# Attention kernel: P V of a group of heads in one block instead of two, and other tiles moved by ScalarE

## The reference

```
q = layer_norm(x) @ wq + bq;  k = ctx @ wk + bk;  v = ctx @ wv + bv      # 16 heads of 32
s = (q . k) / sqrt(32), with -inf where the key's position is behind the query's
o = softmax(s) @ v;  x1 = x + o @ wo + bo
out = x1 + gelu(layer_norm(x1) @ w1 + b1) @ w2 + b2                      # 512 -> 2048 -> 512
```

## Time and profile before

| | us |
|---|---|
| median of 3 runs | 2786.91 (2784.9 to 2787.2) |
| the profiled execution, its own time | 2783.56 |
| its span | 2781.8 |
| TensorE busy | 2739.5 (98%) |
| TensorE weight loads busy | 2501.3 (90%) |
| VectorE busy | 2016.4 (72%) |
| ScalarE busy | 1674.5 (60%) |
| GpSimd busy | 362.6 (13%) |
| mean granted TensorE clock | 0.997 of full |

### The profile page before, as it was taken

One profiled execution on the slowest core, in us unless ns is written; L12 is line 12 of the kernel. 1 busy time (PEld: TensorE's weight loads), 2 busy tenths in 40 slices (PEclk: granted clock), 3 DMA queues, 4 the chain that ended last, 5 costly groups with the idle time before them and its releaser, 6 DMA issues.

```text
span 2781.8 us, 65798 instructions
## 1 busy us (share of the span) xinstructions
PE 2739.5 (98%) x22056; PEld 2501.3 (90%) x22056; DVE 2016.4 (72%) x4853; ACT 1674.5 (60%) x4049; POOL 362.6 (13%) x362
## 2 busy tenths in 40 slices
PE   8999999999999999999979999999998999999999
PEld 7888888888888888888869999999998999999999
DVE  7777777777777776777688787787778666566556
ACT  5766667666676666766666556556556444444444
POOL 2222222221232212322110000000000000000000
PEclk9999999999999999999999999999999999999999
DMA  5333233332333323333243534434435433343342
GB/s 186 119 133 128 98 124 121 132 126 100 124 121 130 124 105 121 119 130 127 100 163 130 196 130 164 189 130 172 182 127 206 157 143 137 134 166 136 120 159 99
DMA packets 153018, 383.03 MB, mean 138 GB/s; under 512 B 13440, under 2 KB 17536, under 8 KB 144768
## 3 DMA queue, kind: packets, MB, share of 16 engines
q1 hardware_dynamic: 152960, 382.28, 37.0%
HBM read 172.51 MB, written 109.05 MB: 101 GB/s over the span
## 4 chain that ended last, share of the span: by engine, by line
PE 95%; DVE 2%; issue 1%; ACT 1%; DMA 0%; POOL 0%; SPq 0%; DVEq 0%; ACTq 0%; POOLq 0%
PE bank_d L478 19%; PE bank_t L505 11%; PE bank_d L473 6%; PE bank_s L1247 6%; PE bank_s L1248 6%; PE bank_s L1249 6%; PE bank_s L493 6%; PE bank_v L528 5%; PE bank_d L1247 5%; PE bank_d L1249 5%; PE bank_d L1248 5%; PE bank_v L1247 2%; PE bank_v L1248 2%; PE bank_v L1249 2%; PE bank_t L1247 1%
## 5 line engine op out<-in xcount | busy, mean ns | idle before, releaser
L824 ACT ACTIVATE sm<-sm,mins 128x128 f32<-128x128 f32 (+3 forms) x1024 | 572.1, 559 | 428.7 <-DVE mins L650 423.5
L650 DVE CUSTOM_DVE_ANT_0 sm<-bank_s,mask 128x128 f32<-128x128 f32 (+3 forms) x1024 | 475.2, 484 | 95.3 <-PE bank_s L493 92.9
L595 DVE COPY pT<-bank_t 128x384 f32<-128x384 f32 (+1 forms) x544 | 307.4, 565 | 230.8 <-PE bank_t L505 230.8
L1247 PE MATMUL bank_s<-w_hi,a_hi 128*128 128x256 f32 x1536 | 435.9, 284 | 3.5 <-DVE a_lo L1373 3.5
L1248 PE MATMUL bank_s<-w_lo,a_hi 128*128 128x256 f32 x1536 | 435.3, 283 | 0.0
L1249 PE MATMUL bank_s<-w_hi,a_lo 128*128 128x256 f32 x1536 | 435.3, 283 | 0.0
L505 PE MATMUL bank_t<-ident,sm 128*128 128x128 f32 x2560 | 412.4, 275 | 8.2 <-ACT pT L595 3.7
L505 PEld LDWEIGHTS bank_t<-ident,sm 128*128 128x128 f32 x2560 | 307.1, 140 | 88.5 <-issue 32.4
L1247 PE MATMUL bank_d<-b_hi,w_hi 128*128 128x256 f32 x1280 | 368.8, 288 | 14.3 <-ACT g L1674 7.0
L1249 PE MATMUL bank_d<-b_hi,w_lo 128*128 128x256 f32 x1280 | 363.6, 284 | 0.0
L1248 PE MATMUL bank_d<-b_lo,w_hi 128*128 128x256 f32 x1280 | 363.3, 284 | 0.0
(11 more groups left out here) (158 smaller groups left out, 6371.2 us busy)
## 6 DMA issues: line engine op xcount, KB each, us to landing
stack<-st_hi SPq DMA_DIRECT2D x256, 256.0 KB, 2.4
stack<-st_lo SPq DMA_DIRECT2D x128, 256.0 KB, 2.4
xr<-x_scratch SPq DMA_DIRECT2D x64, 512.0 KB, 4.2
b_scratch<-b_hi SPq DMA_DIRECT2D x16, 1792.0 KB, 9.1
b_scratch<-b_lo SPq DMA_DIRECT2D x16, 1792.0 KB, 12.8
b_hi<-b_scratch SPq DMA_DIRECT2D x16, 1792.0 KB, 7.4
b_lo<-b_scratch SPq DMA_DIRECT2D x16, 1792.0 KB, 11.1
xt<-in_x SPq DMA_DIRECT2D x64, 256.0 KB, 2.6
```

The source lines that it names most:

```text
L595: copy(out, src).then_inc(moved[n % 2], 1)
L650: op = V.tensor_tensor_reduce(sm[:, n % SLOTS_S, off:off + w], bank_s[n % BANKS_S][:, off:off + w], mask[:, 512 - w:512], 1.0, 0.0, ALU.ad ...
L824: op = A.activation(row, row, ACT.Exp, bias=mins[:, g % 2, c:c + 1], scale=-1.0, accum_out=sums[:, g % 2, c:c + 1])
L1247: pe.matmul(o, lh, rh, start=opens, stop=False, skip_group_check=True)
```

## The change

P V of both pairs of group g is issued in step 3 of group g+1, behind the step's dense matmuls and ahead of its transposes. No matmul is added or dropped. The block needs tile 11, the last of its group, whose transposes are in step 2 and whose move is at the beginning of VectorE's or ScalarE's step 3. ScalarE now moves tiles 3, 5, 9 (3, 5, 7, 9 in group 2) and VectorE the others, tile 11 among them.

```diff
-ACT_MOVES = [(5, 9, 11), (5, 9, 11), (3, 5, 7, 9, 11), (5, 9, 11)]
+ACT_MOVES = [(3, 5, 9), (3, 5, 9), (3, 5, 7, 9), (3, 5, 9)]
...
-    R_AT, PV1_AT, PV0_AT, O_PROD_AT, O_HIGH_AT, O_HIGH_LATE = 4, 5, 9, 6, 7, 11
+    R_AT, PV_AT, O_PROD_AT, O_HIGH_AT, O_HIGH_LATE = 4, 3, 6, 7, 11
...
                     for job, i, j in steps:
                         dense_step(it, job, g, i, j)
-                    if k == PV1_AT and not (it.first and g == 0):
+                    if k == PV_AT and not (it.first and g == 0):
+                        pv(it, g - 1, 0)
                         pv(it, g - 1, 1)
-                    if k == PV0_AT and not it.tail:
-                        pv(it, g, 0)
                     if n >= LAG and not it.tail or n < LAG and not it.first:
                         p_transpose(it, n - LAG)
```

## The result

The changed kernel takes 2819.06 us (median, 2816.67 to 2819.47) against 2787.05 for the one before: 1.0115 of it, 95% interval 1.010 to 1.013. Forecast were 2812 us, in a range of 2784 to 2826. Spans of the profiled executions: 2815.0 and 2781.8, so 33.2 us are to be found. In a trace of any of these kernels the first score stands either some 32.5 or some 36 us after the start (32.6 before, 32.5 in the changed kernel, 36.4 in e8), and the run times fall into two such groups some 3 us apart, so that where few us matter I compare executions with the same start.

What follows compares the result with a forecast made beforehand. TensorE was taken to set the time, with VectorE and ScalarE nearly as full in places. 19.9 + 2 + 3 = +25 us on the profiled 2783.6, 3.4 below the median 2786.9, gave 2812 us, range 2784 to 2826.

Steps and rivals of the forecast that it cites:

- The saving of 0.30 us a block: On TensorE, each P V block costs 0.30 us whatever its size; one fewer a group, -19 us over 16 batches.
- The rival that made a time of the saving alone: Whole kernel: the fixed block cost goes and the cover holds, 2786.9 - 19, so 2768 us; chance 0.15.
- Groups 2 and 3: Middle batches: VectorE's queue behind the block delays masks 8 and 7, +1.05 us in group 2, +0.87 in group 3.
- Groups 0 and 1: Middle batches: the gain of 0.30 us each is kept, 0.1 charged in group 0: -0.20 and -0.30.
- The new wait on tile 11: Step 3: the block needs tile 11 moved; covered by 0.8 us, without cover up to 0.7 a group.
- The tail: After the last scores: tile 11's move stands behind VectorE's normalisations and weight pieces, product at 1420.7, not 1418.27: +2.4 us.
- Move 0.6, 0.1, second part of P V 1.5, 0.2 to the product: Tail: times in us from tile 11's move to VectorE's product, which would start at 1420.7, not 1418.27.
- Batch 0: First batch: group 1 lacks the O products, +1; group 0 sheds 0.9; groups 2 and 3 as elsewhere: +2 us.
- The last batch's: Last batch: groups 0 to 2 -0.9 us; group 3, without dense work, +1.5, estimated between 0.87 and 2.45.
- The sum: Whole kernel: 19.9 for 14 middle batches, 2 for batch 0, 3 for last batch and tail: +25 us.

Runs made afterwards that it cites:

- e8: Changed kernel with VectorE's moves of tiles 0, 1 and 2 cut to 128 of 384 columns (results not the attention's): 2802.4 us, 1.0058 of the kernel before.
- e7: Kernel before with one P V block more a group, pair 1 cut into halves in steps 5 and 6: 2800.7 us, ratio 1.0056.
- e10: Kernel before with the moves of tiles 0, 1 and 2 cut to 128 of 384 columns (results not the attention's): 2783.6 us, ratio 0.9996.
- e2: Changed kernel with the old list of ScalarE's tiles (tile 3 on VectorE, tile 11 on ScalarE): 2830.4 us, 1.016 of the kernel before.
- e1: Kernel before with only the new list of ScalarE's tiles, P V staying in steps 5 and 9: 2786.5 us, ratio 1.0002.
- e3: Changed kernel with tile 11 moved by ScalarE in the tail alone: 2811.1 us, 1.0095 of the kernel before.

## Why the prediction was right, and where it was off

- **The saving of 0.30 us a block** was right in size (e7; group 1 of the changed kernel). The Trainium skill, "TensorEngine Tiling (Array Packing)", section Key Properties, says that a change of tiling mode drains TensorE; e7 agrees in sign, and no run here shows that the drain is the reason. The rival that made a time of the saving alone, 2768, was 51 us off: the saving is on TensorE's queue, and in half of the groups that queue isn't what ends last.
- **Groups 2 and 3** of batch 7 were right to 0.02 us, in place as in size (over the 14 middle batches +1.04 and +0.93 on average). What binds is VectorE's work between the block and mask 7 or mask 8. e8 shortens that work alone and groups 2 and 3 follow; e10 shows that it is nearly free with two blocks; e2 adds one move and groups 0 and 3 follow by that move.
- **Groups 0 and 1** were right: -0.14 and -0.29 for -0.20 and -0.30.
- **The new wait on tile 11** did not bind in the loop: tile 0's transposes come 4.10 after score 3, forecast 4.08. It bound in the tail.
- **The tail is the term that was mis-sized**: +7.2 us for +2.4. The move behind the weight pieces was foreseen. But the 2.4 are how much later VectorE's product would start, and that is not what the O products wait for: they stand in TensorE's queue behind P V, which before started as soon as ScalarE had moved the tile, and so 4.0 us sooner than now. The step "Move 0.6, 0.1, second part of P V 1.5, 0.2 to the product" was off for the product too, which came 5.4 us late: the second part of P V took 2.72 at the lower clock, and R, which stood ahead of it in step 5 of the tail, now stands behind it, so that ScalarE's copy of R comes last and the product 1.8 after P V. On TensorE's path the lower clock is 1.1 of the 7.2 and R 0.9; e1 has the wait and the clock without R behind the block (+6.2), e3 has neither the wait nor the clock (+0.6).
- **Batch 0** was 1.5 us worse than forecast: its group 1, taken as +1, was +1.8, and its group 0, taken as -0.9, was -0.3.
- **The last batch's** +1.5 in group 3 was an estimate between 0.87 and 2.45, and the clock had a part in it: right partly by luck.
- **The sum** was 25 us and the spans differ by 33.2: 4.8 of the missing 8 are the tail, 1.9 the 14 middle batches (1.56 each for 1.42), 1.5 batch 0. All three misses have one sign, and the range covered them.

## What to carry to other kernels

Merging blocks on the busiest engine takes a fixed cost away, but the engines that work for it stand idle beside the long block and miss that time in the steps that became short: add up each helper's queue from the block to the next place that waits for it, and set that against what the busy engine's own queue now leaves. An instruction that moves to another engine must be looked up in that engine's queue in every copy of the loop, the tail too: one copy of 0.6 us behind 4.3 us of other work cost some 6 us there (5.5 by e3, 6.2 by e1).

## What the runs showed of the hardware

A wait of TensorE costs more than itself when the clock falls: in the tails of the changed kernel and of e1 the same 32 records of P V took 2.72 and 3.14 us, at a mean granted clock of 0.59 and 0.50, after idle times of 3.86 and 4.03 us; in the loop, at clock 1.00, they take 1.65. In e3's tail, without that idle time, the clock stayed at 1.00. In the changed kernel's last batch it was 0.50 from 1432.1 to 1438.8 without any such wait (the longest of the 12 us before was 0.76); the kernel before kept 1.00 there. Waits of 0.19 to 0.68 us in the loop of the changed kernel left the clock at 1.00. The loss of the loop has no part in this: it is waits alone.
